# Identity products on TensorE between the expert blocks and the second attention, and in its first batch

## What is computed

```python
x = x + jnp.tanh(g_xattn[0]) * _L0_xattn_ref(ctx_2048, _layernorm(x), mask_BxS2_ik0, L0_xattn_b)
x = x + jnp.tanh(g_ffn[0]) * _L0_ffn_ref(_layernorm(x), ...)
x = x + jnp.tanh(g_xattn[1]) * _L1_xattn_ref(_layernorm(x), ctx_2048, ...)
x = x + jnp.tanh(g_ffn[1]) * _L1_ffn_ref(_layernorm(x), ...)
```

```python
qkv = (x @ w_qkv.T).reshape(B, N, 3, H, D)
k = jnp.concatenate([extra_k, k], axis=2)
attn = jax.nn.softmax(jnp.einsum('bhnd,bhmd->bhnm', q * scale, k), axis=-1)
out = jnp.einsum('bhnm,bhmd->bhnd', attn, v)
```

## Time and profile before

| | us |
|---|---|
| median of 3 runs | 1510.43 |
| lowest and highest | 1507.5, 1512.0 |
| the profiled execution's own time | 1510.48 |
| its span, first to last instruction | 1508.7 |
| PE busy | 1351.8 (90%) |
| DVE busy | 858.4 (57%) |
| ACT busy | 700.8 (46%) |
| POOL busy | 544.2 (36%) |

### The profile page before, as it was taken

One profiled execution on the slowest core, in us unless ns is written; L12 is line 12 of the kernel. 1 busy time (PEld: TensorE's weight loads), 2 busy tenths in 40 slices (PEclk: granted clock), 3 DMA queues, 4 the chain that ended last, 5 costly groups with the idle time before them and its releaser, 6 DMA issues. The chain is left out here.

```text
span 1508.7 us, 31115 instructions
## 1 busy us (share of the span) xinstructions
PE 1351.8 (90%) x8093; PEld 1066.5 (71%) x8093; DVE 858.4 (57%) x2366; ACT 700.8 (46%) x1871; POOL 544.2 (36%) x620
## 2 busy tenths in 40 slices
PE   4989997999999999999446799999998899999998
PEld 3876665777777777777234577676765789999997
DVE  6869982333333333333237467667678576666666
ACT  2443332444444444444124577677776444444443
POOL 1002554333333333333384467666562011111110
PEclk8967998999999999999767899999999999999999
DMA  4025103777666656643441122221120000000000
GB/s 105 0 79 145 33 15 94 213 208 214 204 180 196 192 159 187 203 149 114 119 129 55 50 60 64 57 67 52 44 86 22 15 8 15 15 14 14 14 7 15
DMA packets 107712, 136.14 MB, mean 90 GB/s; under 512 B 29843, under 2 KB 91635, under 8 KB 107603
## 3 DMA queue, kind: packets, MB, share of 16 engines
q1 hardware_dynamic: 64643, 61.15, 13.9%
q0 software_dynamic: 15456, 48.62, 12.0%
q10 hardware_dynamic: 27504, 25.05, 4.9%
HBM read 102.75 MB, written 32.01 MB: 89 GB/s over the span
## 5 line engine op out<-in xcount | busy, mean ns | idle before, releaser
L1259 PE MATMUL ps<-wgu,xT 128*128 (+1 forms) x892 | 310.1, 471 | 2.4 <-ACT xT L1041 1.2
L783 POOL DMA_INDIRECT xg<-n_rows,idx x191 | 181.1, 948 | 295.2 <-DVE wS L2075 208.4
L1259 PE MATMUL ps<-wdn,hT 88*128 (+1 forms) x892 | 228.9, 382 | 2.8 <-DVE hT L2081 1.9
L2235 DVE TENSOR_REDUCE nmx<-ps 128x1 f32<-128x333 f32 x256 | 127.1, 498 | 124.3 <-PE ps L1259 108.6
L1259 PEld LDWEIGHTS ps<-wgu,xT 128*128 128x128 f32 x892 | 155.9, 194 | 54.8 <-issue 6.1
L1137 ACT ACTIVATE pD<-ps,nmx 128x333 f32<-128x333 f32 x256 | 139.2, 546 | 96.7 <-DVE nmx L2235 73.0
L1259 PEld LDWEIGHTS ps<-wdn,hT 88*128 88x128 f32 x892 | 153.7, 191 | 17.5 <-issue 2.7
L2078 DVE TENSOR_TENSOR hC<-sg,ps 128x176 f32<-128x176 f32 x191 | 64.5, 338 | 174.1 <-ACT sg L1092 159.5
L2081 DVE COPY hT<-ps 88x256 f32<-88x256 f32 x191 | 80.3, 420 | 134.1 <-issue 80.8
L1551 PE MATMUL ps<-ident,pD 128*128 128x128 f32 x768 | 131.3, 281 | 27.3 <-DVE pT L2241 16.4
L800 POOL DMA_INDIRECT yg<-y_rows,slotG x128 | 123.2, 963 | 89.8 <-ACT pD L1137 33.4
(11 more groups left out here) (305 smaller groups left out, 3001.2 us busy)
## 6 DMA issues: line engine op xcount, KB each, us to landing
y_rows<-yC ACTq DMA_DIRECT2D x191, 128.0 KB
wgu<-in_wgu SPq DMA_DIRECT2D x64, 352.0 KB
wdn<-in_wdn SPq DMA_DIRECT2D x64, 176.0 KB
xg<-n_rows,idx POOLq DMA_INDIRECT x191
kraw<-in_kD SPq DMA_DIRECT2D x8, 308.0 KB
x<-in_x SPq DMA_DIRECT2D x4, 512.0 KB, 4.9
n_rows<-nB SPq DMA_DIRECT2D x4, 512.0 KB, 3.4
xg<-n_rows SPq DMA_DIRECT2D x16, 128.0 KB, 2.1
```

The source lines that it names most:

```text
L783: pool.indirect_dma_start(out=xg[:, b % XS, :], out_offset=None, in_=n1_rows, in_offset=bass.IndirectOffsetOnAxis(ap=idx[:, b:b + 1], axis ...
L1259: return pe.matmul(o, lhsT, rhs, start=start, stop=stop, **kw)
L2235: dve.tensor_reduce(nmx[:, k:k + 1], ps[:, score_bank(k), 0:NK1], AX, ALU.max, negate=True).then_inc(d_mx, 1)
```

## The change

Three places in PE's list get products of the identity matrix with itself, `ident` (128 x 128, `f32`) times two copies of it side by side, 256 columns. Their results land in PSUM banks and are overwritten later; nothing reads them. Behind the last expert block, before the wait for `d_zero`, a hardware loop of 16 rounds makes 8 products each, 128 in all. Ahead of unit 4 of batch 0 (j == U_ROWS) stand 10 products. In each of the 32 steps of batch 0 one product stands between the wait for the free bank and the wait for the exponentials, and for that the two waits of `d_transpose` change places, in all batches. The instruction lists of ACT, DVE, POOL and SP are the same as before.

```diff
             pe.wait_ge(const_ready, 2)
+            two_idents = ident[:].unsqueeze(1).broadcast_to([P, 2, P])
+
+            def keep_busy(bank, n):
+
+                for _ in range(n):
+                    mm(ps[:, bank, 0:2 * P], ident[:], two_idents, True, True)
...
                     if isinstance(b, int) and b == 0:
+                        if j == U_ROWS:
+                            keep_busy(bank, 10)
                         pe.wait_ge(r_done, 2)
                         pe.wait_ge(d_el, 1 + m)
...
             def d_transpose(b, k):
+                after(pe, d_eva if k % 2 else d_evd, H1 * b + k // 2)
+                if isinstance(b, int) and b == 0:
+                    keep_busy(5 + k % 2, 1)
                 pe.wait_ge(d_exp, STEPS * b + k + 1)
-                after(pe, d_eva if k % 2 else d_evd, H1 * b + k // 2)
...
+            with pe.Fori(0, 16) as i:
+                keep_busy(3, 8)
             pe.wait_ge(d_zero, ZERO_PIECES + 1)
             for j in range(UNITS):
                 d_unit(0, j)
```

## The result

The changed kernel takes 1546.97 us (median of 4 runs, 1542.54 to 1547.32) against 1509.59 us for the kernel before in the same comparison (1507.5 to 1512.0). The ratio of the comparison is 1.0229, with a 95% interval of 1.0213 to 1.0246: 34.6 us or 2.3% slower (the two medians by themselves lie 37.4 us apart). The direction was forecast; the forecast time (1528.8) and the upper end of its range (1538) were too low. The profiled execution took 1542.54 us (span 1540.8), which is 32.1 us above the profiled one of before.

A forecast was written before the change was run, and what follows sets the result against it. PE sets the pace where it works without a gap, but is idle or slow some 100 us around the change. Loop 19.5, units -2.5 and batch 0 +1.3 give +18.3 us on 1510.48: 1528.8 us, range 1517 to 1538.

The forecast's parts named there:

- The loop is longer than the gap: PE's wait for `nS`, 733 to 769 us: the loop is 1.5 times as long, 36 us free, 19.5 us paid.
- The loop's term, +19.5 us: Loop behind the last expert block: 128 x 0.433 = 55.4 us from 733.5, so transposes of `nS` start 19.5 us later.
- signs of being wrong: Idle before the transposes of `nS`, a clock of 0.5 in the loop, or batch 0 under 60 or over 80 us.
- No price for the branches: The loop's 16 branches: nothing taken, since an earlier loop in the trace shows no idle time between records.
- Units, -2.5 us: Transposes of `nS` to ACT's first exponential: 19.7 us at full clock with the 10 products, against 22.2 before.
- Batch 0, +1.3 us: The 32 steps of batch 0: 7.3 us of products on the path less 6 from the clock, between -6 and +14.
- Hidden loop: Rival: products in the loop cost under 0.28 us, so it ends before `nS`; 1503.5 us, or 1508 at 0.28; chance 0.05.
- The stalls go: Rival: batch 0's waits vanish through POOL's lead of 19 us, clock holds, another -10 us, 1519 us; chance 0.1.
- The loop costs twice: Rival: the clock falls in the loop, 128 products take 111 us, another 55 us, to 1584 us; chance 0.03.

The follow-up runs named there:

- e0_changed: The changed kernel run again, nothing altered, in the upper level: 1546.58 us, ratio to before 1.0228.
- b_before: The kernel before, unchanged, run for its trace in the upper level: 1513.69 us (one run).
- e1_loop_only: Changed kernel without the 10 products and the 32 in the steps, only the loop of 128, lower level: 1506.22 us, ratio to before 1.0108.
- e4_written_out: Changed kernel with the 128 products written out instead of the hardware loop, lower level: 1515.15 us, ratio to before 1.0165.
- e11r_thin_gathers: Changed kernel with gathers and sums of batches 0 and 1 for 16 of 128 rows, second try, lower level: 1513.43 us, ratio 1.0161.
- b2_before: The kernel before, unchanged, run for its trace in the lower level: 1491.91 us (one run).

## Why the prediction was right in direction and missed in size

**The loop is longer than the gap, and its excess is paid one for one: right.** No idle stands before the transposes of `nS`, in all kernels with the full loop.

**The loop's term, +19.5 us: the step that failed.** It was 128 x 0.433 = 55.4 us for the loop, less the gap. It measured +34.6 in the first pair of profiles and +33.4 in the second (e0_changed against b_before). The price of a product was right: 0.432 us each (e1_loop_only, e4_written_out, e11r_thin_gathers). What failed is the step from the price to the loop's length. The sum took 128 products back to back; in the upper level, three of them take 12 us. The low clock around it and at the start adds 2 to 4 us. The forecast named as signs of being wrong a clock of 0.5 in the loop, and the windows show it there. In the lower level the same term is +19.5 to +19.9 us. The whole change costs 24.6 us there (written out), inside the forecast's range of +7 to +28, and the upper level without its 13.5 us (68.84 instead of 55.33 in e0_changed) would come to some +21, an estimate by subtraction. The trace of before may have had a sign of it, which I used only for a rival: the pause of 3.33 us on PE marked "issue" in the earlier trace rows, and the remote ones on ACT. I had read them as single events tied to their places. The same kernel in the lower level (b2_before) has no such wait of over 0.9 us from 735 to 935 us, on PE, ACT or DVE, and is 20 us faster.

**No price for the branches: right.** 55.33 us with 16 branches and 55.33 written out; the slow stretch stands in both. By the Trainium skill's rule on taken branches to code outside the fetched window (page "Runtime: NRT & Kernel Launch", section "Instruction fetch mechanics"), named in the prediction, the loop could have been longer; with this short body these runs show no such cost.

**Units, -2.5 us: right,** -2.7 and, in the second pair, -2.6. The sum of 19.7 us for them was 19.56, and the pause on ACT fell beside the ten products as supposed. The comparison was against 22.2 us that held a pause; against the lower level's 18.5 us the same 19.6 is a loss of 1.1: the ten products cost 4.3 us there, more than the 3.2 us of the clock. So there is luck in it: the pause in the kernel before made room for them.

**Batch 0, +1.3 us: right,** +2.2 and +3.0, and +1.6 to +1.9 in the lower level. Hidden products and a better clock nearly balance 13.8 us of products. The 1.0 us between first exponential and batch 0 was counted in neither term.

**The rivals.** Hidden loop: refuted, the columns cost the full f32 pace. The stalls go: refuted, batch 0 still has waits of 4.0 and 4.7 us on ACT and is longer, not shorter. The loop costs twice: its mechanism exists, a clock at 1.2 GHz under dense products for some 3 us and slow issue besides, at a quarter of the price it was given. That is the part of the range that was missing: I gave the loop's term no spread at all, though it was the largest, and all the spread to batch 0.

**What stays open.** What the slow stretch is. Shown: it is tied to the level of the runs, not to the chip (chip 9 had both levels, and chip 2); not to the branches; it ends some 3 us behind the last gather of batch 0 wherever the loop starts. Shown too: no transfer of instructions runs in it or ends it, and gathers beside PE are not enough to bring it. Argued only: that it is of a kind with the pauses marked issue and remote that the upper level has in the kernel before. Whether it needs the gathers' transfers, or a shortage of instructions of another kind, was not settled, since both tests met the lower level. Open as well is why POOL's first gather starts 1.4 to 2.1 us later in every kernel with products in the gap.

## What to carry to other kernels

An operation that only keeps an engine busy stands in order like any other: price it by its columns at the type's pace from a row, multiply, and hold the sum against the gap; what is over is paid in full, and what ended 9.75 us ahead of the gap's end was worth nothing here. Tie it to a signal near the end of the gap (here DVE's sums, 6 to 8 us before the data) and not to a count from its start; sixteen products did for the units what 128 did (15.3 us both). Even so the gain in time was lost: sixteen gave +0.6 us and twelve -1.6. And give the largest term of a sum a spread of its own when the trace shows pauses without a cause nearby: here the gain of the best version, 1.6 us, is under a tenth of what two levels of the same kernel differ by.

## What the runs showed of the hardware

The same kernel on the same chip ran at 1490 us or 1512 us in different groups of runs. From the transposes of `nS` to the first exponential the lower level takes 18.5 us and batch 0 58.4, the upper 22.1 and 69.0; the upper has waits marked issue and remote there, which the lower lacks. That they make up the whole difference was not shown.

Dense full-f32 products right behind real work, with 0.9 us of idle between, ran at 1.2 GHz for some 3 us in one execution (0.56 and 0.50 granted from 734 to 737) and at full clock throughout in another (1.00 from 731 to 786): a dense stream alone does not promise the clock.

PE slowed to one instruction in 0.70 us or a multiple of it for 12 us, with no wait in its text there, in each of the three profiled executions with the full loop (or its products written out) in the upper level, and in none of the six in the lower. In no trace that has it did a transfer of instructions run in that time.
